# A graph-attention stack on one core: the features of one normalisation turned by VectorE and a trip through DRAM, not by TensorE

## What is computed

```python
h = relu(layernorm(x));  x = x + attention_6_heads(h, Wq, Wk, Wv, Wf, adj)
h = relu(layernorm(x));  x = x + graph_attention_12_heads(h, W, w_src, w_dst, H_w, adj)
h = relu(layernorm(x));  x = x + attention_6_heads(...)
h = relu(layernorm(x));  x = x + graph_attention_12_heads(...)

# graph attention: t = h @ W;  z = leaky(tanh(t) @ w_src + (tanh(t) @ w_dst).T), -999 where no edge
#                  f = elu(softmax(z) @ t + b);  g = sigmoid(h @ H_w.T + H_b);  out = g*f + (1-g)*h
```

## Time and profile before

| | |
|---|---|
| time, median of 3 runs | 2075.15 us (2074.44 to 2075.71) |
| the profiled execution: its own time | 2070.91 us |
| its span in the trace | 2069.1 us |
| TensorE's mean granted clock | 0.989 |
| PE busy | 1999.1 us (97%) |
| ACT busy | 1955.6 us (95%) |
| DVE busy | 1836.3 us (89%) |
| POOL busy | 1588.7 us (77%) |

### The profile page before, as it was taken

The page is one execution under the profiler, slowest core; times in us unless marked ns, Lnnn a source line. Parts: engine busy times, 40 slices in busy tenths (PEclk is TensorE's granted clock), DMA queues, the critical chain, the costliest instruction groups (busy, mean ns, idle before and its releaser), DMA issues.

```text
span 2069.1 us, 58618 instructions
## 1 busy us (share of the span) xinstructions
PE 1999.1 (97%) x19596; PEld 1847.7 (89%) x19596; DVE 1836.3 (89%) x4117; ACT 1955.6 (95%) x6800; POOL 1588.7 (77%) x2874
## 2 busy tenths in 40 slices
PE   6899999999999999999999999999999999999974
PEld 6899999998899999999999999999999999999963
DVE  5589899899899999999999999999999999999875
ACT  5699999999999999999999999999999999999985
POOL 5567888888887777777777777777777777777764
PEclk9999999999999999999999999999999999999997
DMA  5012222323222222223331221222221212211112
GB/s 165 13 41 65 71 71 74 77 69 80 72 79 78 52 53 56 52 58 88 107 105 49 55 58 48 56 56 52 53 56 51 59 50 54 59 49 51 42 39 62
DMA packets 309219, 130.64 MB, mean 63 GB/s; under 512 B 229430, under 2 KB 308668, under 8 KB 308924
## 3 DMA queue, kind: packets, MB, share of 16 engines
q1 hardware_dynamic: 308924, 126.90, 23.6%
HBM read 69.42 MB, written 57.41 MB: 61 GB/s over the span
## 4 chain that ended last, share of the span: by engine, by line
PE 55%; POOL 20%; ACT 13%; DVE 5%; issue 5%; DMA 2%; SPq 1%; POOLq 0%; DVEq 0%; ACTq 0%
PE psum L744 23%; PE psum L754 11%; ACT LG L515 6%; PE psum L831 3%; ACT LA L509 3%; POOL prod L427 3%; PE psum L842 3%; DVE LG L635 3%; PE psum L853 2%; PE psum L736 2%; PE psum L819 2%; DVE neg_max L639 2%; PE psum L771 2%; PE psum L871 2%; POOL rstd L370 2%
## 5 line engine op out<-in xcount | busy, mean ns | idle before, releaser
L515 ACT ACTIVATE LG<-LG,neg_max 128x128 f32<-128x128 f32 x1536 | 596.2, 394 | 21.8 <-DVE neg_max L639 21.4
L509 ACT ACTIVATE LA<-LA,neg_max 128x128 f32<-128x128 f32 x768 | 299.3, 411 | 0.0
L515 ACT ACTIVATION_READ_ACCUMULATOR LG<-LG,neg_max 128x1 f32 x1536 | 296.4, 193 | 0.0
L427 POOL TENSOR_TENSOR prod<-th,vec 128x384 f32<-128x384 f32 x256 | 256.1, 1024 | 20.3 <-ACT th L556 20.2
L635 DVE COPY_PREDICATED_SCALAR LG<-no_edge,no_edge_score 128x1536 f32 x128 | 254.3, 1987 | 4.5 <-ACT LG L547 4.2
L639 DVE TENSOR_REDUCE neg_max<-LG 128x12 f32<-128x1536 f32 x128 | 224.4, 1753 | 14.1 <-DVE LG L635 0.5
L406 POOL TENSOR_SCALAR ey<-y 128x384 f32<-128x384 f32 x128 | 64.8, 507 | 203.5 <-DVE y L687 203.5
L423 POOL TENSOR_TENSOR ey<-ey,hG 128x384 f32<-128x384 f32 x128 | 131.6, 1028 | 91.0 <-ACT ey L550 91.0
L754 PE MATMUL psum<-hT_hi,qk_lo 128*128 128x256 f32 x1152 | 199.4, 281 | 0.0
L754 PE MATMUL psum<-hT_lo,qk_hi 128*128 128x256 f32 x1152 | 198.8, 281 | 0.0
L754 PE MATMUL psum<-hT_hi,qk_hi 128*128 128x256 f32 x1152 | 198.6, 281 | 0.0
(11 more groups left out here) (125 smaller groups left out, 6252.0 us busy)
## 6 DMA issues: line engine op xcount, KB each, us to landing
context<-gcT SPq DMA_DIRECT2D x512, 48.0 KB, 2.1
back<-context SPq DMA_DIRECT2D x128, 192.0 KB, 2.4
xin<-x SPq DMA_DIRECT2D x64, 192.0 KB, 2.6
x_mid<-x SPq DMA_DIRECT2D x64, 192.0 KB, 1.9
xin<-x_mid SPq DMA_DIRECT2D x64, 192.0 KB, 2.6
out<-x SPq DMA_DIRECT2D x64, 192.0 KB, 1.9
ahead<-stage SPq DMA_DIRECT2D x16, 288.0 KB, 3.3
stage<-w_vf SPq DMA_DIRECT2D x8, 288.0 KB, 4.1
```

What stands on the lines that cost most here:

```text
L427: last = pool.tensor_tensor(prod[:, i, :], th[:], vec[:, r.pair(k - 2), 2 + i, :], ALU.mult)
L509: last = act.activation(head, head, ACT.Exp, scale=-1.0, bias=neg_max[:, 0, h:h + 1], accum_out=rsum[:, h:h + 1])
L515: last = act.activation(head, head, ACT.Exp, bias=neg_max[:, 1, a:a + 1], accum_out=den[:, a:a + 1])
```

## The change

The turn of `hM` leaves PE. DVE turns it in 32x32 blocks inside SBUF (`hM_turned`), SP writes it in four DMAs to a DRAM tensor `features_T` that puts the blocks in their places, waits for them, and reads it back as `hM_back`. POOL, not ACT, takes the ReLU from `hM_back` and rounds to `hT_hi`. DVE forms `hT_lo` from `hM_back`, which is in SBUF, where it was in PSUM before. The core of the diff:

```diff
+            def features_back(g):                                       # SP
+                b = g % 2
+                sp.wait_ge(s["m_turn"], g + 1)
+                if g >= 1:
+                    sp.wait_ge(s["m_lo"], g)
+                rows = features_T[b].rearrange("(j a) (c i b) -> i a c j b", a=32, i=4, b=32)
+                for i in range(4):
+                    sp.dma_start(rows[i], hM_turned[32 * i:32 * i + 32, :].rearrange("p (c j b) -> p c j b", c=KC, j=4)).then_inc(s["m_out"], 16)
+                sp.wait_ge(s["m_out"], 64 * (g + 1))
+                sp.dma_start(hM_back[:], features_T[b]).then_inc(s["m_back"], 16)
...
+                if r.has(k + 7):                                        # POOL, step
+                    pool.wait_ge(s["m_back"], 16 * r.done(k + 7))
+                    wait_latest(pool, r, ("m_v", k + 3))
...
+                    pool.tensor_scalar(hT_hi[:, :, (k + 7) % 4, :], hM_back[:].rearrange("p (c n) -> p c n", c=KC), 0.0, None, ALU.max).then_inc(s["m_hi"], 1)
...
-                if r.has(k + 4):                                        # ACT, step
-                    act.wait_ge(s["m_hT"], r.done(k + 4))
-                    act.activation(hT_hi[:, :, (k + 4) % 4, :], chunks(bank(2)), ACT.Relu).then_inc(s["m_hi"], 1)
...
+                if r.has(k + 8):                                        # DVE, step
+                    if r.has(k + 7):
+                        dve.wait_ge(s["m_out"], 64 * r.done(k + 7))
+                    dve.wait_ge(s["m_h"], r.done(k + 8))
+                    dve.transpose(hM_turned[:], hM[:]).then_inc(s["m_turn"], 1)
+                if r.has(k + 7):
+                    dve.wait_ge(s["m_hi"], r.done(k + 7))
+                    dve.scalar_tensor_tensor(hT_lo[:, :, (k + 7) % 4, :], hM_back[:].rearrange("p (c n) -> p c n", c=KC), 0.0, hT_hi[:, :, (k + 7) % 4, :].bitcast(F32),
+                                             ALU.max, ALU.subtract).then_inc(s["m_lo"], 1)
...
-                if r.has(k + 4):                                        # PE, step
-                    pe.wait_ge(s["m_h"], r.done(k + 4))
-                    wait_latest(pe, r, ("g_haug", k - 3), ("m_lo", k + 3))
-                    features(hM, bank(2)).then_inc(s["m_hT"], 1)
```

More of the change, by code:

```diff
@@ new lines, in step @@
+                if r.has(k - 1):
+                    pool.wait_ge(s["g_th"], r.done(k - 1))
+                    for i in range(2):
+                        last = pool.tensor_tensor(prod[:, i, :], th[:], vec[:, r.pair(k - 1), 2 + i, :], ALU.mult)
+                    last.then_inc(s["g_prod"], 1)
+                if r.has(k - 4):
+                    pool.wait_ge(s["y_exp"], r.done(k - 4))
+                    pool.tensor_tensor(ey[:], ey[:], hG[:, (k - 4) % HELD, :], ALU.subtract).then_inc(s["ey_f"], 1)
@@ L483, in setup @@
             def setup(k):
[L484 removed]
+                for pair, at in ((0, -2), (1, 0)):
                     if k == at:
@@ new lines, in step @@
+                if r.has(k + 1):
+                    pe.wait_ge(s["g_h"], r.done(k + 1))
+                    wait_latest(pe, r, ("z_leaky", k - 1), ("g_lo", k))
+                    features(hG[:, (k + 1) % HELD, :], bank(5)).then_inc(s["g_hT"], 1)
+                if r.has(k + 3):
+                    pe.wait_ge(s["p_norm"], r.done(k + 3))
+                    wait_latest(pe, r, ("g_gate", k), ("gpt0", k - 2), ("pt", k + 2))
+                    wait_latest(pe, r, ("x1", k + 1), ("pt", k + 2))
+                    for i in range(MH):
+                        last = pe.transpose(bank(2 + i // KC)[:, (i % KC) * N:(i % KC + 1) * N], LA[:, i * N:(i + 1) * N], idf[:])
+                    last.then_inc(s["pt_ps"], 1)
@@ new lines, in step @@
+                if r.has(k + 1):
+                    weights("gate", k + 1)
+                    pe.wait_ge(s["g_lo"], r.done(k + 1))
+                    wait_latest(pe, r, ("gpt0", k - 1), ("pt", k + 3), ("g_gate", k))
+                    pe.matmul(bank(2)[:, 0:D], ones[:], hb3[:, r.pair(k + 1), :], start=True, stop=False)
+                    nodes_times(bank(2)[:, 0:D], g_hi, g_lo, hg_hi, hg_lo, D, begun=True).then_inc(s["g_gate_ps"], 1)
+                if r.has(k + 6):
+                    weights(f"c{(k + 4) % 2}0", k + 6 - (k + 4) % 2)
+                    wait_latest(pe, r, ("gpt2", k - 1), ("s_max", k + 4), ("qk0", k + 5))
+                    queries_keys(k + 4, 0, bank(7)).then_inc(s["qk_ps0"], 1)
@@ new lines, in step @@
+                if r.has(k + 5):
+                    weights("V", k + 5)
+                    pe.wait_ge(s["m_lo"], r.done(k + 5))
+                    wait_latest(pe, r, ("z_leaky", k), ("g_sdR", k), ("s_max", k + 4), ("m_val", k + 4))
+                    b = (k + 5) % 4
+                    nodes_times(bank(6)[:, 0:D], lambda c: hT_hi[:, c, b, :], lambda c: hT_lo[:, c, b, :], vf_hi, vf_lo, 0).then_inc(s["m_v"], 1)
+                if r.has(k + 1):
+                    weights("h", k + 1)
+                    pe.wait_ge(s["g_lo"], r.done(k + 1))
+                    wait_latest(pe, r, ("g_haug", k))
+                    nodes_times(bank(1)[:, 0:D], g_hi, g_lo, hg_hi, hg_lo, 0).then_inc(s["g_h_ps"], 1)
```

606 lines of the change are left out of this document (287 added, 319 removed).

## The result

The changed kernel takes 2169.09 us (median of 4 runs, 2165.15 to 2170.16), the kernel before 2074.8 beside it: a ratio of 1.0451 (95% interval 1.0436 to 1.0467), 4.5% slower. The forecast was 2108, slower, in a range up to 2160.

The account below looks back on a forecast made before the run. It took PE as the bound before, and a two-step circle through the DMA trip after: + 17 late, + 9.5 split, + 8 start on the profiled 2070.9 gave 2105, predicted as 2108 us against the median, range 2040 to 2160.

Parts of the forecast that it names:

- the circle: Late steps: `sd`, `gcT`, DMA trip, `hM_back`, `prod`, `sd`; 31.25 us over two steps, 15.6 a step; chance 0.50.
- the start: First graphs: each needs its own trip, and trips can't overlap; + 8 us, between 0 and + 20.
- GpSimd's ReLU: ReLU moved from ACT to POOL, priced as its `gate` operation: 0.51 us, bounds 0.46 and 1.2.
- VectorE's lock: DVE instructions with two SBUF inputs and POOL's SBUF reads exclude each other: 0.5 us a step, bounds 0 and 1.6.
- if the ReLU on GpSimd takes over 1 us: Sign that the prediction is wrong, listed under what the changed profile would show; the ReLU was priced at 0.51 us.
- the trip: SP's second DMA trip, from `gcT` until `hM_back` has landed: 12.0 us, bounds 10.9 and 14.
- The turn from SBUF: DVE's added 128x384 turn: taken as 0.49 us, the same as from PSUM, bounds 0.4 and 0.57.
- The factor of 19: Skill's warning that a plain DMA with transposing strides is 19 times slower than the hardware's path; given no chance.
- PE's 15.10: Late period PE would allow after losing three of six transposes: 15.43 - 0.33 us.
- The split: 28 steps in which the second pair's weights are split: 16.1 us a step against 15.76.
- Rival 2: Lock becomes the bound, `hT_lo` and `LA` behind POOL's full sums: period 16.2 late, 16.7 split, 2179 us; chance 0.10.
- Rival 1: PE stays the bound and gives its 0.33 us back: 2048 us, faster; chance 0.32.

Follow-up runs that it names:

- the sum later: Changed kernel with GpSimd's sum of `xin` and the bias behind the layernorm's three small instructions: 2148.77 us; with the ReLU on ScalarE too: 2056.11 us.
- its cheap form: Changed kernel with GpSimd's ReLU written as min with 3e38, then max with 0 (also "min and max"): 2136.47 us.
- the runs with eight instructions: Changed kernel with eight GpSimd instructions of 128x384 added behind its last, in different operations and outputs: 2176.05 us, a single run.
- the full interleaving: Changed kernel with all four writes of `features_T` issued ahead of SP's wait for `context`: 2140.39 us.
- all three edits: Changed kernel with the ReLU on ScalarE, GpSimd's sum behind the small layernorm instructions and all four `features_T` writes ahead of `context`'s wait: 2164.57 us.

## Why the prediction was wrong in its range

The step that failed is the pricing of the circle's parts and of the start, not the circle. The forecast took GpSimd's ReLU at 0.51 us and it took 1.19; it took VectorE's lock at 0.5 us a step and it was 1.1; it took the start at + 8 and it was + 24. The first alone decides about the range: the kernel with the ReLU at 0.51 us takes 2136.5 us, inside it. The prediction had named "if the ReLU on GpSimd takes over 1 us" as a sign of being wrong.

**Right.** What bounds the kernel before, and the mechanism: the circle sd, gcT, trip, ReLU, prod over two steps. It was put at 31.25 us and is 31.65 in the alternating pairs (31.9 from the rows above, which is also twice the mean late period). That it came so near is in part luck: the trip was put 0.4 us too long, and the parts of DVE and GpSimd 0.4 and 0.65 too short (14.9 for 14.5, 5.4 for 4.75). GpSimd waits ahead of L459 and DVE at `sd`, as said. The turn from SBUF takes 0.49 us of DVE, 1505.80 to 1506.29 by the timeline, as taken from PSUM. The trip was put at 12.0 and is 11.6. The four writes that do the turning land in 2.1 us by the page, as `context`'s do. The factor of 19 of the Trainium skill (VectorE: DVE Perf Modes, The three transpose paths) is not seen at runs of 32 elements. The page gives it for a large innermost stride of the destination, a condition that the prediction left out and that these writes don't meet. PE's 15.10 was right: the kernel with the ReLU on ScalarE and the sum later has 15.07.

**Mis-sized terms**, which together take the sum from 34.5 to 97.8 us:

1. The ReLU: 0.51 taken "as its `gate` operation of like shape", 1.19 measured. The bound above, 1.2, stood beside it, but the sum used the low end; the same shape is not the same operation. The edit of this term alone is 33 us.
2. The lock: "I take 0.1 each, 0.5 together". Measured: 0.85 for the second `y`, 0.18 for `hT_lo` in the mean, 0.05 for `LA`, 1.1 together. A price for an average phase was wrong, since the phase is fixed by the order: the sum on GpSimd and the `y` both start behind the same `sd`, and meet at full length in each of the 83 late steps (1.40 to 1.42 us). `hT_lo` with both inputs in SBUF does join the lock: 0.86 at 1522.23, beside GpSimd's `prod`, where it takes 0.52 at 1506.29. The rule of the Trainium skill (SBUF — State Buffer, Who interferes with whom) holds here for the new form too.
3. The late period was put at the circle's mean, 15.6. But a step takes the longer of circle and DVE's own time, and those that get a long trip (up to 14.1 to the issue, where the mean is 9.2) are not paid back: 15.95 by the starts, 0.1 over half of the alternating pair.
4. The split: 16.1 taken, 16.57 measured. I take it for terms 1 to 3 again with the split's piece on top, which no run shows apart; with the ReLU on ScalarE it is 15.50.
5. The start: "I put + 8 us, between 0 and + 20", it is + 24, outside its own bounds. The first trips are strictly one after the other, 8.4 us each: SP issues the writes at 23.12, 31.54 and 39.97, while the first group, behind the loads of weights, took 5.23 us to land by the chain of work. PE's 20.4 us of waits for `hM` gave way to 42.1 us for `hT_lo` in the same 90 us. Only 12 us of it go with the ReLU.

Beside these terms the forecast overlooked how full GpSimd itself is. It put GpSimd at 12.4 us of a step; by period less waits it is 15.0, level with DVE's 15.2. Of the 2.6 us, 0.7 are the ReLU and 1.2 the short gaps between instructions, which busy time leaves out. Much of the rest is in instructions that run longer beside DVE's, as `no_edge` with 1.00 for 0.30 at 1505.03, beside DVE's scaling of `LA`.

Rival 2 (2179) is near in time, but not the cause: it wanted `hT_lo` and `LA` behind GpSimd's full sums, and these have 0.18 and 0.05 us of lock. The lock alone gives DVE 15.3, and taking it from the second `y` gave 20 us, taking the ReLU off GpSimd 88. Rival 1 decides below 12.35 us of trip and lock above plain work; it took the ReLU on another engine and the sum elsewhere to reach its time (2056 for 2048).

What stays open: how much of the loss is the turn and how much the new orders. No kernel with the new orders and PE's turn was run. Open too: what GpSimd's full queue adds to the circle in the changed kernel, since every edit that took the ReLU or its price away relieved both.

## To carry to other kernels

Off-loading the busiest engine pays only what the next circle of waits leaves: write down each circle that a DMA trip closes, with the queue's other trips in it, before counting what the engine saves. Look for slack before you put a wait for a DMA on a queue: the same ReLU cost 88 us more on GpSimd, ahead of its products, than on ScalarE, and still 55 us more in its cheap form. Take an engine's own time as its period less its waits, since its busy share can hide that it is full. And price a GpSimd operation by its own operations and their order, not by its shape.

## What the runs showed of the hardware

- GpSimd on 128x384 fp32 (the runs with eight instructions and with min and max): min then max and multiply then add 0.51 us, a cast 0.50, max alone and add alone 1.16 to 1.19, max then min 1.49, whether the output is fp32r or fp32, strided or not.
- A VectorE instruction with two SBUF inputs that starts 0.01 us behind a GpSimd sum of 1.01 us takes 1.41 us, in the changed kernel. Moving the sum by three short instructions gives 0.56, and the price shows up at another pair (0.89 for 0.56).
- Two DMA trips in one queue can't both be first: the full interleaving took GpSimd's wait for the trip from 26.3 us to 0.8 and put 10.1 us of waits on `back`, 33.6 us when all three edits were in (1200 to 1800 us).
